# Token embedding by one product of 128 rows per tile, with the first norm in quarters, in a two-layer vision transformer kernel

## What is computed

```python
Ws = [(idx0, W0, b0, PRE[0]), (idx1, W1, b1, PRE[1]), (idx2, W2, b2, PRE[2])]
outs = [_level(x, idx, W, b, p, GP) for idx, W, b, p in Ws]
n_tokens = outs[0].shape[1]
outs = [outs[0]] + [_interp_linear(o, n_tokens) for o in outs[1:]]
y = jnp.concatenate(outs, axis=-1)
return y @ Wf.T + bf
...
qkv = jnp.einsum('bsd,ed->bse', x, wq_in)
```

## Time and profile before

| | |
|---|---|
| median of three runs | 999.29 us (998.73 to 1000.45) |
| span of the profiled execution | 1014.8 us, 19178 instructions |
| device time of that execution alone | not listed |
| busy in the span | PE 743.6, DVE 697.2, ACT 672.0, POOL 345.9 us |
| the block `embed` | from the start to about 103 us |

### The profile page before, as it was taken

One profiled execution on the slowest core, in us unless ns is written; L12 is line 12 of the kernel. 1 busy time (PEld: TensorE's weight loads), 2 busy tenths in 40 slices (PEclk: granted clock), 3 DMA queues, 4 the chain that ended last, 5 costly groups with the idle time before them and its releaser, 6 DMA issues. The chain is left out here.

```text
span 1014.8 us, 19178 instructions
## 1 busy us (share of the span) xinstructions
PE 743.6 (73%) x7062; PEld 537.8 (53%) x7063; DVE 697.2 (69%) x1403; ACT 672.0 (66%) x1229; POOL 345.9 (34%) x260
## 2 busy tenths in 40 slices
PE   2987373344299547999997488867775898999985
PEld 1464141122277324589996444324444467899974
DVE  4159998999599888745443475986998875444542
ACT  1267956999799657755554369578983661676663
POOL 6620460000000000357776424580001202477763
PEclk9979555555599768999999879555556798999999
DMA  5224485000121318623333456380003942233332
GB/s 168 71 90 130 138 234 169 1 23 1 47 75 69 122 45 289 200 54 59 57 56 47 90 233 254 117 297 35 2 2 105 344 169 71 37 54 58 59 45 32
DMA packets 61883, 105.26 MB, mean 104 GB/s; under 512 B 9678, under 2 KB 43618, under 8 KB 61554
## 3 DMA queue, kind: packets, MB, share of 16 engines
q1 hardware_dynamic: 45426, 87.77, 25.6%
q0 software_dynamic: 16384, 16.53, 10.4%
HBM read 76.39 MB, written 27.87 MB: 103 GB/s over the span
## 5 line engine op out<-in xcount | busy, mean ns | idle before, releaser
L2301 DVE COPY m_xgT<-m_px 128x768 f16<-128x768 f16 (+1 forms) x46 | 22.9, 497 | 123.5 <-PE m_px L2146 123.5
L2268 ACT ACTIVATE m_pu<-m_pu,m_b,m_unit 128x256 f32<-128x256 f32 (+1 forms) x138 | 63.5, 509 | 60.9 <-PE m_pu L2178 58.4
L2309 DVE SCALAR_TENSOR_TENSOR m_hT<-m_pu,m_unit,m_hT 128x512 f16<-128x512 f32 (+1 forms) x138 | 86.4, 663 | 17.4 <-ACT m_hT L2261 17.2
L1084 ACT ACTIVATE a_ex<-m_pieces,a_nb 128x256 bf16<-128x256 f16 x192 | 94.6, 560 | 5.4 <-DVE a_nb L1110 5.4
L922 PE MATMUL a_pp<-a_room 16*128 16x256 bf16 x240 | 56.1, 412 | 39.8 <-DVE m_pieces L1098 31.9
L2272 ACT ACTIVATE m_pu<-m_pu,m_unit 128x512 f32<-128x512 f32 (+1 forms) x69 | 41.1, 597 | 62.7 <-PE m_pu L2178 61.7
L2261 ACT ACTIVATE m_hT<-m_pu,m_unit 128x512 f16<-128x512 f32 (+1 forms) x138 | 81.6, 636 | 0.0
L2112 POOL DMA_INDIRECT m_xg<-xn_d,m_token x70 | 70.0, 1000 | 32.1 <-issue 20.6
L2120 POOL DMA_INDIRECT out_h<-m_yo,m_token x39 | 62.1, 1593 | 40.6 <-DVE m_yo L2319 28.8
L2120 POOL DMA_INDIRECT h_d<-m_yo,m_token x39 | 62.1, 1592 | 37.3 <-DVE m_yo L2319 18.0
L2178 PE MATMUL m_pu<-m_xgT,m_w 128*128 128x256 f16 (+1 forms) x690 | 70.4, 261 | 1.3 <-DVE m_xgT L2301 1.3
(11 more groups left out here) (488 smaller groups left out, 1914.2 us busy)
## 6 DMA issues: line engine op xcount, KB each, us to landing
m_pieces<-in_m_w SPq DMA_DIRECT2D x11, 768.0 KB, 5.1
a_early_w<-in_m_w SPq DMA_DIRECT2D x10, 768.0 KB
hv_raw<-in_m_w SPq DMA_DIRECT2D x8, 768.0 KB, 6.2
w1h_d<-hv_parts SPq DMA_DIRECT2D x8, 768.0 KB, 4.1
m_w<-w1h_d SPq DMA_DIRECT2D x8, 768.0 KB, 9.0
m_pieces<-in_m_w SPq DMA_DIRECT2D x8, 576.0 KB, 5.3
a_room<-in_m_w SPq DMA_DIRECT2D x8, 576.0 KB, 3.6
hv_raw<-in_m_w SPq DMA_DIRECT2D x8, 576.0 KB, 5.9
```

The costliest lines, as they stand in the source:

```text
L1084: last = act.activation(ex[:, n % 2, r], v16t[:, n, r, :], ACT.Exp, bias=nbt[:, n, r:r + 1], scale=scale, accum_out=sumst[:, n, r:r + 1])
L2268: act.activation(pu[:, u, n, q * w:(q + 1) * w], pu[:, u, n, q * w:(q + 1) * w], ACT.Relu, bias=b1[:, bass.ds(e * FC + 2 * n + q, 1)], sca ...
L2309: last = v.scalar_tensor_tensor(hT[:, u, 1, third], pu[:, u, n, 0:2 * w], unit[:, 1:2], hT[:, u, 0, third], ALU.mult, ALU.subtract)
```

## The change

It does seven things, all in `embed`:

1. One product per tile. The stationary operand is `lt`: 128 rows, of which 48 are the tile's pixels, 16 the interpolation weights of level 2 (`up2`, put beside the pixels in `r0` before the turn, so that they come out with them), and 64 those of level 1 (`up1`, by four DMAs). For odd images the two 64-row parts change places. The moving operand is `zz` (128 x 192 per image, in the second half of `vf`). The base products, `z`, `up`, `bias`, `o1`, `o2`, `f0`, VectorE's adds and one copy per pair are gone.
2. Level 1 is multiplied with `w1f` = W1 Wf straight to 192 columns, two images a product (eight products of 96 x 128), in place of two of 512 columns. Levels 0 and 2 go through `seg` (W0 and level 2's tokens, 128 rows) in eight products of 64 columns.
3. The bias is summed by two products into `zb`, and VectorE adds it to level 1's part (L801).
4. The norm comes in quarters (`aggregate`, `normalise` of four tiles), with statistics directly on ScalarE's copy.
5. `HOLDS` is gone.
6. ScalarE's list is rearranged: three totals ahead of the mixing copies, three behind them, and chunk 0's and 1's copies between the quarters.
7. VectorE's maxima are moved among the quarters. TensorE's turns and chunks stand whole, in the order of before.

```diff
-                HOLDS = {6: (turned, 4), 10: (summed, 2), 20: (mixed, 4), 24: (turned, 6), 26: (fused, 4)}
...
+                for half in range(2):
+                    for rows, first in ((slice(EMB, P), 0), (slice(0, EMB), 1)):
+                        sp.dma_start(lt[rows, half, first:B:2, :], a["up1"][:, half:half + 1, :]
+                                     .to_broadcast([EMB, B // 2, P])).then_inc(raised, 16)
...
                 def fuse(half, m, bank):
-                    pe.wait_ge(kept, 5 + 2 * half + m // 2)
                     for j in range(2):
-                        last = nc.tensor.matmul(bank[:, j * D:(j + 1) * D], f0[:, half, 2 * m + j, :], wz[:],
+                        b = 2 * m + j
+                        last = nc.tensor.matmul(bank[:, j * D:(j + 1) * D], lt[:, half, b, :], zz[:, b, :],
                                                 start=True, stop=True)
                     last.then_inc(fused, 1)
...
+                for n in range(2):
+                    for k in range(4):
+                        r0_, j = EMB * (k % 2), k // 2
+                        last = nc.tensor.matmul(pt[r0_:r0_ + EMB, n, j * D:(j + 1) * D], seg[:, 4 * n + k, :], wfe[:],
+                                                start=True, stop=True)
+                    last.then_inc(mixed, 1)
+                pe.wait_ge(widened, 1)
+                nc.tensor.transpose(po[:, 3, 3 * P:3 * P + 2], wide[:], c.ident[0:2, 0:2]).then_inc(crossed, 1)
+                turn_pixels(0, pt[:, 2])
+                pe.wait_ge(raised, 64)
+                pe.wait_ge(lower, 1)
+                pe.wait_ge(upper, 1)
                 for m in range(4):
...
+                    pe.wait_ge(shifted, m // 2 + 1)
+                    pe.wait_ge(zkept, m // 2 + 1)
+                    if m == 3:
+                        pe.wait_ge(bkept, 1)
                         pe.wait_ge(proj.weighed, 1)
...
+                for n in range(3):
                     weigher.total(act, n)
...
+                for n in range(2):
+                    act.wait_ge(mixed, n + 1)
+                    for first in range(2):
+                        rows = slice(first * EMB, (first + 1) * EMB)
+                        last = act.activation(zz[rows, 4 * n + first:4 * n + 4:2, :], pair(pt[rows, n]), ACT.Copy)
+                    last.then_inc(zkept, 1)
...
+                for n in range(3, 6):
                     weigher.total(act, n)
...
+                pixels(0, pt[:, 2])
+                for m in range(3):
+                    keep(0, m, po[:, m])
                 root(0)
...
+                keep(0, 3, po[:, 3])
+                x_high(0)
+                x_high(1)
+                root(1)
+                x_copy(0)
+                x_copy(1)
+                take(0, 0, 2)
+                x_high(2)
+                x_high(3)
+                x_copy(2)
+                x_copy(3)
+                take(0, 2, EACH)
+                pixels(1, pt[:, 0])
+                take(1, 0, 2)
...
+                def measure(half, m):
+                    dve.wait_ge(hkept, 4 * half + m + 1)
                     for j in range(2):
                         t = 2 * (2 * m + j) + half
                         last = v.bn_stats(st[:, t, :], c.h[:, t, :])
...
+                measure(1, 0)
+                measure(1, 1)
+                aggregate(2)
+                measure(1, 2)
+                normalise(2)
+                measure(1, 3)
+                aggregate(3)
+                peaks_of(0, 4, EACH)
+                normalise(3)
                 x_low(4)
                 x_low(5)
...
+                peaks_of(1, 0, 4)
                 x_low(6)
                 x_low(7)
```

More of the change, by code:

```diff
@@ L550, in _ @@
-                last.then_inc(summed, 1)
+                pe.wait_ge(wkept, 1)
+                for m in range(4):
+                    if m % 2 == 0:
+                        pe.wait_ge(kept, m // 2 + 1)
+                    for k in range(2):
+                        last = nc.tensor.matmul(po[:, m // 2, (m % 2) * D:(m % 2 + 1) * D],
+                                                f1[:, k, 2 * m * 64:(2 * m + 2) * 64], w1f[:, k, :],
+                                                start=(k == 0), stop=(k == 1))
+                    if m % 2:
+                        last.then_inc(summed, 1)
@@ L662, in keep_base @@
-                def keep_base(n):
-                    half, m = n // 4, n % 4
-                    act.wait_ge(based, n + 1)
-                    act.activation(tiles[:, half, 2 * m:2 * m + 2, :], pair(po[:, m]), ACT.Copy).then_inc(hkept, 1)
-                for n in range(4):
-                    keep_base(n)
-                pixels(0)
-                for n in range(2, 4):
+                for n in range(2):
+                    act.wait_ge(mixed, n + 1)
[3 more added lines that the diff above has]
+                    last.then_inc(zkept, 1)
@@ L671, in _, with keep @@
+                def keep(half, m, bank):
+                    act.wait_ge(fused, 4 * half + m + 1)
+                    act.activation(tiles[:, half, 2 * m:2 * m + 2, :], pair(bank), ACT.Copy).then_inc(hkept, 1)
+                for n in range(3, 6):
                     weigher.total(act, n)
-                for n in range(4, 8):
-                    keep_base(n)
+                pixels(0, pt[:, 2])
+                for m in range(3):
+                    keep(0, m, po[:, m])
                 root(0)
-                for g in (0, 2):
-                    x_high(g)
-                    x_high(g + 1)
-                    x_copy(g)
-                    x_copy(g + 1)
@@ L680, in _ @@
-                take(0, 0, EACH)
-                pixels(1)
-                for n in range(4, 6):
-                    weigher.total(act, n)
-                take(1, 0, 3)
-                root(1)
-                take(1, 3, EACH)
-                for g in (4, 6):
-                    x_high(g)
-                    x_high(g + 1)
-                    x_copy(g)
-                    x_copy(g + 1)
+                keep(0, 3, po[:, 3])
+                x_high(0)
+                x_high(1)
+                root(1)
@@ new lines, in _ @@
+                x_copy(0)
[8 more added lines that the diff above has]
+                take(1, 0, 2)
+                for m in range(3):
+                    keep(1, m, pt[:, BANK[m]])
+                root(2)
+                keep(1, 3, pt[:, BANK[3]])
+                take(1, 2, 4)
+                root(3)
@@ L692, in _ @@
+                x_high(4)
+                x_high(5)
+                take(1, 4, EACH)
+                x_high(6)
+                x_high(7)
+                for g in range(4, 8):
+                    x_copy(g)
                 take(2, 0, EACH)
@@ L788, in _ @@
                 order_pixels(0)
[L789 to L799 removed]
+                raise_pixels(0, pt[:, 2])
+                measure(0, 0)
@@ new lines, in _ @@
+                measure(0, 1)
+                aggregate(0)
+                measure(0, 2)
+                normalise(0)
+                measure(0, 3)
+                aggregate(1)
+                x_low(0)
+                x_low(1)
+                normalise(1)
+                x_low(2)
+                x_low(3)
+                x_peak(0)
+                order_pixels(1)
+                peaks_of(0, 0, 2)
+                raise_pixels(1, pt[:, 0])
+                peaks_of(0, 2, 4)
+                measure(1, 0)
```

267 lines of the change are left out of this document (118 added, 149 removed).

## The result

The changed kernel takes 1008.65 us (median of 13 runs, 1003.97 to 1014.4), the kernel before 1001.19 us in the runs beside them (13 runs, 995.9 to 1004.88). The ratio is 1.0092, with an interval of 1.0070 to 1.0113: slower by 0.9%. The forecast was 997.1 us, range 993.5 to 1001.5, with 0.24 on slower. It was wrong in sign.

The account below looks back on a forecast made before the run. The first block's end was taken as the bound, two chains ending within 0.2 us, TensorE pacing before chunk 0. Summed steps ended it at 100.7 instead of 102.9, 2.2 us off 999.29: 997.1 us, range 993.5 to 1001.5.

Parts of the forecast that it names:

- the reference: First profile of the kernel before, span 1014.8 us; its block's forecast saving was applied to the runs' median, 999.29.
- The sum's end of the block: First 105 us: SP's landing of the spaced q and k copies moves from 102.7 to 100.7 us.
- The steps between the milestones: First whole product at 47.2 us, chunks 0, 1, 2 at 58.9, 71.7, 83.7, last `x_low` done at 87.5.
- the inversion: Between chunks 0 and 1, chunk 0's first two products and a copy precede `x_high` 2; 12.8 us against 9.7 before.
- 8.3 early: Chunk 0 starts at 58.9 instead of 67.21 us; chunks 1 and 2 then only 5.2 and 3.1 early.
- Level products and mixing: TensorE before the pixel products: level 1 4.9 us, level 2 3.67, mixing 5.6; done at 37.4 with a clock rise.
- The totals as the gate: ScalarE's six weight totals delay the first pixel copy to 47.2 us; VectorE would be ready at 42.8.
- `up1`'s DMAs: Four more DMAs ahead of the weights delay level 2's gathers by 1.3 us, from 21.74 to 23.0.
- All later code is the same and starts with this end: Behind the block: the rest of the program shifts with the block's end, 2.2 us less.
- The stall comes again: Rival, chance 0.20: the 2.65 us "remote" stall recurs or was that execution's only, so that gain is missing; 999.7 us.
- The clock is lost: Rival, chance 0.22: low clock in chunks 0 and 1 and the rows' turns; at most 3.1 us slower, 1001.5 in part.
- Concurrent products: Rival, chance 0.05 with pacing gathers: mixing products in different column groups overlap; either gives some 3 us more, 994.3.

Follow-up runs that it names:

- E1: The kernel before, file unchanged, profiled a second time; its lifting copy, the end of the block, starts at 90.95 us.
- E7: The change plus 162 already-met waits on TensorE, 81 more instructions, so its stream is as long as before's; ratio 1.0043 to the kernel before.
- E2: The change with ScalarE's weight totals back at their old places; ratio 1.0072 to the kernel before.
- E4: The change with the block's last lifting copy made three times instead of once; ratio 1.0118 to the kernel before.
- E5: The change with ScalarE's copies reordered at two places to follow TensorE's order; ratio 1.0001 to the kernel before.
- E6: The change with TensorE's queue put in the order in which ScalarE copies; ratio 0.9979 to the kernel before.

## Why the prediction was wrong

**The step that failed is the reference.** "The span of this profile is 1014.8; no device time of that execution alone is listed, and the 999.29 is the median of three runs. I apply the difference to that". The profiled execution was slower than the runs by some 17 us, and 12.0 us against E1 lay in the very block whose end was forecast. The sum's end of the block, 100.7, was only 3.3 us above what was measured; set against a usual execution's 90.95 it would have read 9.7 us later, some 1009 us. That this meets the measured 1008.65 is partly luck: the block really ended 6.5 us later, and 2.4 us that the sum did not have came behind it. The forecast was 0.2% faster, measured was 0.9% slower, a miss of 11.4 us, and 12.0 of reference, less 3.3, plus 2.4 are 11.1 of it.

**The steps between the milestones** were near: chunk 0 to chunk 1 12.8 forecast and 14.2 measured, chunk 1 to 2 12.0 and 11.4, first whole product to chunk 0 11.7 and 12.1, end of the last `x_low` to the lifting copy 13.2 and 13.4. Even the inversion is in the text, as cost: "Chunk 0's first two products and one copy stand before `x_high` 2". What it lacked was the comparison of the two orders: 9.3 and 9.9 us in E1, of which the change makes 14.2 and 11.4. The "8.3 early" at chunk 0, of which 5.2 and 3.1 were said to be left at the next two, was a gain that a usual execution doesn't show: 54.98 against 55.65, 0.7 early, then 4.2 and 5.7 late.

**Level products and mixing.** W1's products took 4.45 us (4.9 forecast), level 2 1.96 at the high level. Mixing took 1.52 us instead of 5.6 and was done at 32.3 instead of 37.4, below the lower bound of 34.6. The reason to set the Trainium skill's rule aside was wrong, see the last section. The mixing's speed gained nothing, since the next gate, the order of half 0's pixels, lies at 40.20.

**The totals as the gate: wrong, as the text's own test says** ("a first whole product near 43 (the totals no gate)"): 42.92. The sixth total ended at 41.6, and the pixel turns, begun at 40.86, were copied at 42.01, 0.4 us after it: the gathers were the gate, but closely. In E7, where the pixels were ordered at 38.77, the sixth total was the gate, and the first whole product stood at 44.20. In the change the totals acted through the DMA engines, 1.8 us (E2).

**`up1`'s DMAs:** level 2 turned at 22.30, 0.4 us later than in E1, where 1.3 was forecast.

**"All later code is the same and starts with this end":** half right. It starts with it (E4), but it is not the same in time: its place in TensorE's instruction stream moved by 81 instructions, and a code load fell into the weight loads: 2.4 us. No rival spoke of this.

**Rivals.** The stall was indeed of the profiled execution only, as "The stall comes again" has it; it was 2.65 of 12 us. "The clock is lost" fails by its own test, more than half of 58 to 84 at 0.50: it was 7.0 of 26 us. But E1 has none there, so the rival had a part: 1.5 to 2 us of the block's length, as worked out above. From 25 to 100 us the low level adds up to about the same, 28.2 us after the change and 26.5 in E1, only at other places. "Concurrent products" was right on the chip and worth nothing. The lower end of the range, 993.5, does not follow from its terms: 2.8 us and half of 1.7 and 1.3 off 997.1 give 992.8. The 11.7 and 12.8 add up to 11.6 and 12.7.

**The ledger.** Order of the two queues, with the clock's part, +9.0 us (E5, E6 against the change), code load +2.4 (71.54 against 69.16), everything else that the change does -2.5 (E6's 88.40 against 90.95): 8.9 us, and 0.92% of 1001 is 9.2.

## What to carry to other kernels

Before costing a change, compare the profiled execution's span with the times of the runs; if they differ by more than the effect in question, take another profile, or find where they differ, before any milestone of it is used as a reference. Look at the granted clock first: all but the stall of the 12 us here went with it. When work is cut finer on one engine, write the two queues side by side in order: each copy must stand in the order in which its producer makes it, and a finished result behind a wait for a later one costs time at each such place (two places, 9 us here with the clock that went with them). And where two versions differ in the number of instructions ahead of a stretch that is bound by DMA, look where the code loads fall before calling a distant 2 us a cause or a gain.

## What the hardware showed that was not expected

**Column groups do run side by side.** The eight mixing products of the change (128 rows contracted, 64 output columns, alternately in output rows 0 and 64) have sixteen records, which started in pairs 7 ns apart, a pair each 0.163 us: 1.52 us for eight products. In E1, at the same level of the clock, L563 and L565 alternate the column group too, and start 0.45 us apart, one behind the other (0.54 and 0.49 us in its rows). What differs is that those two contract 64 rows and have unlike shapes, 64 x 64 and 64 x 16. The Trainium skill's rule that products with small M in different column groups run concurrently ("TensorE: Matmul & The Clock Gate", section "Why this matters for your kernels") thus holds here, and its page "TensorEngine Tiling (Array Packing)", section "Tiling Modes", has the likely reason for E1: a change of the tiling mode drains the array. No run here tried equal shapes in before's mixing, so that reason is not shown.

**One code load goes with a lag of one DMA engine that is longer than the load.** The q8 load took 1.07 us, but the lag behind the next slowest engine grew from weight load to weight load: 0.9, 1.4 and 2.1 us in the change, 1.4, 2.0 and 3.7 in E5. Why it grows stays open.
